# A gated recurrence: gate biases moved from the activations into one-row matmuls

## What is computed

```
xi, xf, xg, xo = xt @ U_i + b_i, xt @ U_f + b_f, xt @ U_c + b_c, xt @ U_o + b_o
def step(carry, xs):
    h, c = carry
    i_t = sigmoid(xi_t + h @ V_i)
    ...
    g_t = tanh(xg_t + h @ V_c)
    o_t = sigmoid(xo_t + h @ V_o)
    c_new = h * c + i_t * g_t
    h_new = o_t * tanh(c_new)
```

## Time and profile before

| | us |
|---|---|
| time, median of 3 runs | 1961.46 |
| lowest and highest of them | 1950.76, 1961.59 |
| span of the profiled execution, first to last instruction | 1867.1 |
| the recurrence in it, first weight load to last new h | 110.7 to 406 |

### The profile page before, as it was taken

One profiled execution on the slowest core, in us unless ns is written; L12 is line 12 of the kernel. 1 busy time (PEld: TensorE's weight loads), 2 busy tenths in 40 slices (PEclk: granted clock), 3 DMA queues, 4 the chain that ended last, 5 costly groups with the idle time before them and its releaser, 6 DMA issues. The chain is left out here.

```text
span 1867.1 us, 43356 instructions
## 1 busy us (share of the span) xinstructions
PE 1627.8 (87%) x13366; PEld 1314.2 (70%) x13366; DVE 1095.9 (59%) x4199; ACT 998.9 (53%) x3116; POOL 786.7 (42%) x1358
## 2 busy tenths in 40 slices
PE   7978899988859987999998888879999888884995
PEld 5756677767759985788887566679999845553542
DVE  7933433348737777699998755523333377763552
ACT  5854444446636656666665433246666534441663
POOL 6710000014426666111111677745565434554675
PEclk9989999999969999899999799989999989995998
DMA  3200000010014420000000511122222253105331
GB/s 114 84 1 1 1 1 1 1 27 1 1 36 134 123 80 1 2 3 2 2 3 3 156 47 48 62 62 70 72 71 72 56 150 86 58 24 88 100 86 35
DMA packets 125926, 91.76 MB, mean 49 GB/s; under 512 B 23591, under 2 KB 116554, under 8 KB 125701
## 3 DMA queue, kind: packets, MB, share of 16 engines
q1 hardware_dynamic: 109110, 61.89, 12.6%
q0 software_dynamic: 13568, 25.90, 4.3%
q10 hardware_dynamic: 3024, 1.21, 0.4%
HBM read 57.71 MB, written 33.30 MB: 49 GB/s over the span
## 5 line engine op out<-in xcount | busy, mean ns | idle before, releaser
L1361 ACT ACTIVATE FEAT<-BANKS,FEAT 128x128 f32<-128x128 f32 x544 | 155.5, 368 | 82.1 <-PE BANKS L1314 82.1
L1206 POOL DMA_INDIRECT scratch_made<-FEAT x136 | 144.9, 1065 | 122.6 <-DVE FEAT L1500 119.8
L1061 ACT ACTIVATE EXP<-BANKS,NEGMAX 128x128 f32<-128x128 f32 x512 | 139.4, 383 | 59.5 <-DVE NEGMAX L1073 59.5
L440 ACT ACTIVATE gates<-BANKS,EXP 128x64 f32<-128x64 f32 x384 | 97.4, 314 | 112.6 <-PE BANKS L417 112.6
L1314 PE MATMUL BANKS<-FEAT 128*128 128x128 f32 x1088 | 145.5, 277 | 0.0
L1323 PE MATMUL BANKS<-AUX,FEAT 128*128 x1088 | 144.5, 276 | 0.4 <-ACT FEAT L1361 0.4
L417 PEld LDWEIGHTS BANKS<-AUX,EXP 128*128 128x128 f32 x768 | 95.4, 191 | 69.7 <-DVE AUX L464 69.6
L1198 POOL DMA_INDIRECT scratch_sent<-FEAT,POS x128 | 125.1, 977 | 38.3 <-issue 37.5
L990 POOL COPY EXP<-AUX 128x32 f32<-128x32 f32 x256 | 42.5, 211 | 217.8 <-PE BANKS L1036 217.8
L1314 PEld LDWEIGHTS BANKS<-FEAT 128*128 128x128 f32 x1088 | 133.9, 194 | 0.0
L1323 PEld LDWEIGHTS BANKS<-AUX,FEAT 128*128 128x128 f32 x1088 | 133.2, 193 | 0.6 <-issue 0.6
(11 more groups left out here) (367 smaller groups left out, 4196.0 us busy)
## 6 DMA issues: line engine op xcount, KB each, us to landing
EXP<-in_L_ffn_W SPq DMA_DIRECT2D x128, 128.0 KB, 2.1
FEAT<-scratch_sent SPq DMA_DIRECT2D x136, 64.5 KB
EXP<-scratch_made SPq DMA_DIRECT2D x32, 256.0 KB, 3.4
FEAT<-scratch_sent SPq DMA_DIRECT2D x96, 65.5 KB, 1.9
X<-in_x SPq DMA_DIRECT2D x16, 256.0 KB, 2.9
STAGE<-in_adj SPq DMA_DIRECT2D x16, 256.0 KB, 3.3
scratch_sent<-NONE SPq DMA_DIRECT2D x48, 65.5 KB, 3.3
scratch_sent<-FEAT,POS POOLq DMA_INDIRECT x192, 2.3
```

The costliest lines, as they stand in the source:

```text
L440: act.activation(gates[:, at, sp_, :], PS[2 * at + par][:, u * B:(u + 1) * B], f, bias=wr["b" + gate]).then_inc(done, 1)
L1061: last = act.activation(tile(EXS[:, par], 4 * k + n), tile(PS[j], c), ACT.Exp, bias=NEGMAX[:, par, 4 * k + n:4 * k + n + 1])
L1206: pool.indirect_dma_start(out=made2, out_offset=bass.IndirectOffsetOnAxis(ap=XI_I[:, t % R_IN, H:ROW2], axis=0), in_=YO[:, t % R_OUT, :], ...
L1361: last = act.activation(tile(HR[:, t % R_H], c), tile(PS[2 + t % 2], c), ACT.Gelu, bias=BT[:, c, t:t + 1])
```

## The change

The biases are loaded as rows of 128 elements on partition 0. Each `inputs` now issues two matmuls: the one with U, and one with the bias row as weights (1 row, 128 columns) and a row of ones as the moving operand (1 row, 256 columns), which adds the bias to the same 256 columns of the bank. The gate activations have no bias operand. A step that prefetches has one filler fewer, so its number of 256-column matmuls is as before. The initial six `inputs` also become twelve matmuls, without a filler taken away there.

```diff
-            wr["b" + gate] = EXP[:, 6 * H + at:6 * H + at + 1]
+            wr["b" + gate] = EXP[0:1, 4608 + at * H:4608 + (at + 1) * H]
...
-                    sp.dma_start(wr["b" + gate], column(a["L0_ffn_b_" + gate])).then_inc(s.later, 16)
+                    sp.dma_start(wr["b" + gate], a["L0_ffn_b_" + gate].rearrange("(o h) -> o h", o=1)).then_inc(s.later, 16)
...
+                    pe.matmul(PS[2 * gate_at + par][:, part * half:(part + 1) * half].rearrange("p (r h) -> p r h", r=2),
+                              wr["b" + gate], ones[0:1, :].unsqueeze(1).to_broadcast([1, 2, half // 2]), start=False, stop=False,
+                              skip_group_check=True)
...
-                        for _ in range((2 if prefetch and u < 6 else 3) - (step < B)):
+                        for _ in range((1 if prefetch and u < 6 else 3) - (step < B)):
...
-                            act.activation(gates[:, at, sp_, :], PS[2 * at + par][:, u * B:(u + 1) * B], f,
-                                           bias=wr["b" + gate]).then_inc(done, 1)
+                            act.activation(gates[:, at, sp_, :], PS[2 * at + par][:, u * B:(u + 1) * B], f).then_inc(done, 1)
```

## The result

The changed kernel takes 2081.11 us (median of 4 runs, 2070.55 to 2089.34), the kernel before 1958.87 us beside it (4 runs, 1950.76 to 1961.59). The ratio is 1.063, 95% interval 1.060 to 1.066: 6.3% slower. The prediction was 2079, in a range of 1962 to 2105.

The account below looks back on a forecast made before the run. It took one chain of 2.27 us per step to bound the recurrence. Terms of +129 us, mostly from half clock, less three returns gave 117.5 on a base of 1961.5: 2079 us, range 1962 to 2105.

Parts of the forecast that it names:

- What bounds the step: Recurrence: one chain from V matmuls through activations to the new h sets 2.27 us per step, not TensorE's throughput.
- Activations without bias: Gate activations: 84 ns less each; only the c activation counts, once per step, 10.8 us at most over 128 steps.
- Change of rows: TensorE, around each one-row matmul: changing between 128 rows and 1 costs 0.2 us at full clock, 0.3 at half.
- The sign given for it: New profile: weight loads idle by about 0.1 us on both sides of line 410.
- The clock: TensorE: without the filler the clock is 0.50 for most of the first 64 steps; chance 0.45, 2060 to 2105 us.
- The one fall: At 1661.1 to 1664.5 us TensorE is busy 3.40 of 3.40 with one-row matmuls, then 0.50 is granted.
- The rival that it holds: One-row matmuls count like others and the clock holds: +0.8 us, 1962; chance 0.18.
- From the start on: Recurrence: clock at 0.50 from the start, as the initial prefetch begins at 0.50 and is half one-row; +9.4 us there.
- The sum: Recurrence: +9.4 initial prefetch, +85 and +19 first 64 steps, +13 and +2 after, +1 at full clock: +129 us.
- three returns of 4 us: Pairs of steps without prefetch, with two full fillers, may lift the clock for a while: taken off +129, leaving +117 to +118.
- The one with the clock low in parts: Recurrence: the clock returns in every tile and falls again; 25 to 30 slow steps, 2010 to 2025 us; chance 0.33.
- Span against time: Whole kernel: the 94.4 us around the profile's span of 1867.1 are not touched, giving the base of 1961.5 us.

Follow-up runs that it names:

- e2_no_bias: The kernel before with gate activations without bias operand and the bias left out altogether: 1858.03 us against 1867.44, ratio 0.995.
- e3_full_rows: The changed kernel with a bias matmul of 128 rows, 1/128 in the moving operand: 1860.97 us against 1867.44 for the kernel before, ratio 0.996.
- e6_half_rows: The changed kernel with a bias matmul of 64 rows: 1925.53, 1996.33, 1994.48 and 1970.26 us against 1865.73 for the kernel before.
- e9_changed_warm: The changed kernel with twelve fillers between initial prefetch and first step: 2081.44 us against 1959.65 for the kernel before, ratio 1.063.
- e4_one_filler_fewer: The kernel before with one filler fewer in prefetching steps and nothing else of the change: 1909.53 us against 1867.44, ratio 1.022.
- e7_filler_kept: The changed kernel with the filler kept in prefetching steps: 2024.89, 1997.70, 2038.65 and 2042.07 us against 1865.73 for the kernel before.
- e8_filler_kept_warm: The changed kernel with the filler kept and twelve fillers ahead of the first step: 1993.08, 2039.84, 2041.01 and 2038.16 us against 1865.73 for the kernel before.
- e10_half_rows_warm: The changed kernel with a 64-row bias matmul and twelve fillers ahead of the first step: 2018.54, 1982.97, 1973.30 and 2002.01 us against 1959.65 for the kernel before.

## Why the prediction was right, point by point

- **What bounds the step.** Right. e2_no_bias shortens only the activations and the step goes from 2.27 to 2.18 us.
- **Activations without bias**, 84 ns taken of 0 to 97: measured 91 (314 to 223), 11.3 us over 128 steps against 10.8. The copy against which I priced it is 6 ns shorter than an activation without bias (217 against 223), but the row with 97 was the better neighbour, being of the same shape.
- **Change of rows**, 0.2 us at full clock and 0.3 at half. Right in kind: the loads of the bias matmul idle 0.03 us each in e3_full_rows, and 0.33 us for each pair at full clock in the changed kernel and in e6_half_rows. Counted between ends of groups in the earlier trace rows, L1700 ends at 1660.96 + 1.12 = 1662.08, which is 1.05 us after L1678, against 4 x 0.217 = 0.87: 0.18 us extra. L1704 ends 1.09 us after L1700. The 0.43 us of the sum for two passes of 256 columns is twice the 0.217 of the earlier trace rows. That one row takes as long as 128 is shown by the shortest records: 587 ns for 1x512 (L1700) and 592 for 128x512 (L1678) before, 374 for 1x256 (L410) and 379 for 128x256 (L407) after. The steps that contain it: 2.35 expected, 2.36 measured; at half clock 4.04, 3.44 and 4.47 expected against 4.01, 3.41 and 4.43. Prefetching steps with row sum at full clock were to hide it, with 2.14 us of TensorE's time under a chain of 2.18, and do: 2.18 us in the first steps of e9_changed_warm. The sign given for it was wrong in size: the loads idle by 0.33 us ahead of line 410 and of the next line, not by about 0.1, so idle time of the load is not the same as the time that a change adds (0.18 and 0.19 us by the earlier trace rows).
- **The clock.** Right, and with the one-row matmul's own time at half clock it carries nearly all of the loss. The one fall on which I built it had narrow full-row passes beside the one-row matmuls, so it could not name these as the reason by itself; the experiments do. e4_one_filler_fewer shows that the missing filler alone loses the clock, e9_changed_warm that the one-row matmul doesn't replace it, e3_full_rows that it is not missed if the bias matmul has 128 rows. The sentence that the filler "was what held the clock" is too narrow, though: in e7_filler_kept and e8_filler_kept_warm the filler is there and the clock is lost as well, perhaps because the one-row matmuls stretch the step. The rival that it holds, because TensorE stays as busy as before, is out: TensorE is busy for 10.30 of 10.30 us in e9_changed_warm and for 33.79 of 34.10 in e8_filler_kept_warm, and then 0.50 is granted.
- **From the start on.** Right, but it hardly matters: e9_changed_warm starts at 1.00 and is as slow (+121.8 us against +122.2).
- **The sum.** Initial prefetch +9.4 expected, +9.3 measured; steps 0 to 63 +104 (85 + 19), +101.5; steps 64 to 71 +15, +14.8; the rest +1, +1.0. Sum +129, measured 126.6 in the profile and 128.1 on the quicker chip. The deduction of three returns of 4 us was a mistake: there was no return in either profile of the changed kernel. That 117.5 nevertheless comes within 5 us of the 122.2 of the comparison, and 2079 within 2 of 2081, is partly luck: the base of 1961.5 was 2.6 above the later median of before, and the runs on that chip spread over 11 to 19 us.
- **Rivals.** The one with the clock low in parts, at 2010 to 2025, does occur as a pattern of the clock, but with 64 rows or with the filler kept, not with the change as it is.
- **Span against time.** Wrong: the two came from chips on which this kernel differs by 5%. It did no harm only because the difference lies outside the recurrence.

## What to carry to other kernels

A matmul that is there to add a bias can be given all 128 rows (bias on every partition, 1/128 in the moving operand); here that cost no time in any step (2.18 us in e3_full_rows, as without any bias in e2_no_bias). With one row it kept neither the clock (0.50 for the first 70 steps) nor the overlap of the load of weights with the matmul ahead (idle 0.33 us at full clock, 0.65 at half). Where fillers hold TensorE's clock, as here (1.00 with them, 0.50 in most of the first 64 steps of e4_one_filler_fewer), count what takes a filler's place by the rows it has, and look at the granted clock before and after, not at the busy share, which was 100% here in the slow stretches. And look at span against time: here they differed by 1.7 to 2.4 us in each execution that has both, while the 94.4 us ahead of the prediction were between a profile and runs that were not of one execution, and by all signs not of one chip; compare only runs made side by side.

## What the runs showed of the hardware that was not expected

- The cost of changing the number of rows was the same for one row and for 64: with 64 rows the loads idle for 0.33 us as with one (prefetching steps of 2.36 us in both), with 128 rows as the neighbours' by 0.03 us for each load (2.18).
- The same steps of one kernel ran at either clock for tens of microseconds: in e6_half_rows at 3.85 us (123.20 / 32) for 32 steps and then at 2.19 (67.80 / 31) for the next 31, and its four runs spread over 71 us. The clock also fell in a kernel that had begun its steps at 1.00 (e10_half_rows_warm, after 10.3 us). That the longer step at half clock helps to keep it there would fit this, but was not tried.
- Two data-moving layers of the same kernel take about 50 us longer each on one chip than on another (150 against 204 us in one of them), at a lower granted clock (0.98 and 0.83), while the recurrence is the same to 0.2 us (422.0 and 422.2). What is slow on that chip was not tried.
